# First products of a weight folding on both row halves of the matrix array, with one group of output weights moved ahead of the second products

## The reference

```python
q_hk = (hidden_q @ Wq.T).reshape(b, s, H, K)              # H = 16, K = 128
q_big = jnp.einsum('bshk,hkq->bshq', q_hk, w_kc_q)        # q = 192
q_r = jnp.einsum('bshq,hqr->bhsr', q_big, W_qr)           # r = 64
k_r = jnp.einsum('bld,hdr->bhlr', kv_rope, W_kr)          # d = 64
scores = jnp.einsum('bhsr,bhlr->bhsl', q_r, k_r)
attn = jax.nn.softmax(scores, axis=-1)
ctx_c = jnp.einsum('bhsl,bld->bhsd', attn, kv_rope)
ctx_lat = jnp.einsum('bhsd,hkd->bshk', ctx_c, w_kc_kv)
out = ctx_lat.reshape(b, s, H * K) @ Wo.T
```

## Time and profile before

| what | us |
|---|---|
| median of 3 runs | 1159.86 |
| lowest and highest of them | 1150.75, 1166.39 |
| the profiled execution, by the device time | 1156.2 |
| the profiled span | 1154.3 |
| of it, the folding phase | about 21 |

### The profile page before, as it was taken

The page is one execution under the profiler, slowest core; times in us unless marked ns, Lnnn a source line. Parts: engine busy times, 40 slices in busy tenths (PEclk is TensorE's granted clock), DMA queues, the critical chain, the costliest instruction groups (busy, mean ns, idle before and its releaser), DMA issues. The chain is left out here.

```text
span 1154.3 us, 32206 instructions
## 1 busy us (share of the span) xinstructions
PE 1093.3 (95%) x12466; PEld 835.1 (72%) x12467; DVE 707.1 (61%) x1804; ACT 452.4 (39%) x1329; POOL 300.6 (26%) x390
## 2 busy tenths in 40 slices
PE   7898999999999999999978999999998899899996
PEld 6776878878878668988756767767766688556664
DVE  6897755554646475545437888888885687422221
ACT  2453443443435222221135555555642566222221
POOL 1701532323132200000001212212213555334442
PEclk9899999999999999999999999999998999799999
DMA  8631211111111118000202332322324743312221
GB/s 257 185 86 39 74 45 44 54 28 55 27 55 30 35 43 245 1 0 0 50 7 67 78 81 74 87 77 65 92 79 155 210 112 85 102 29 34 37 27 10
DMA packets 72494, 82.55 MB, mean 72 GB/s; under 512 B 28910, under 2 KB 57231, under 8 KB 71916
## 3 DMA queue, kind: packets, MB, share of 16 engines
q1 hardware_dynamic: 64124, 62.33, 20.5%
q0 software_dynamic: 8304, 19.32, 6.4%
HBM read 64.91 MB, written 18.53 MB: 72 GB/s over the span
## 5 line engine op out<-in xcount | busy, mean ns | idle before, releaser
L1775 ACT ACTIVATE xattn_exps<-xattn_ps_s,xattn_top 128x256 f32<-128x256 f32 x256 | 117.8, 475 | 84.9 <-DVE xattn_top L1839 84.9
L776 PEld LDWEIGHTS attn_ps_q<-attn_xnT,w_b_q 128*128 128x128 f32 x1024 | 120.2, 195 | 12.6 <-issue 12.6
L776 PE MATMUL attn_ps_q<-attn_xnT,w_b_q 128*128 128x128 f32 x1024 | 124.8, 278 | 0.0
L830 PE MATMUL attn_ps_out<-w_b_o,attn_oT 128*128 128x256 f32 x480 | 106.6, 380 | 2.6 <-DVE all_x L1011 1.5
L830 PEld LDWEIGHTS attn_ps_out<-w_b_o,attn_oT 128*128 128x128 f32 x480 | 90.0, 190 | 16.1 <-DVE all_x L1011 2.4
L884 ACT COPY attn_qT<-attn_ps_q 128x512 f32<-128x512 f32 x64 | 38.1, 595 | 148.8 <-PE attn_ps_q L776 148.8
L1846 DVE STREAM_TRANSPOSE xattn_expsT<-xattn_exps 128x1024 f32<-128x1024 f32 x64 | 79.5, 1242 | 25.9 <-ACT xattn_exps L1775 25.8
L1836 DVE TENSOR_REDUCE xattn_raw_top<-xattn_ps_s 128x4 f32<-128x1024 f32 x64 | 77.3, 1207 | 15.9 <-PE xattn_ps_s L1666 15.8
L1643 PEld LDWEIGHTS xattn_ps_o<-xattn_xnT,all_d_a 128*128 128x128 f32 x512 | 62.1, 198 | 17.8 <-ACT xattn_exps L1775 7.2
L1608 POOL TENSOR_TENSOR xattn_ctxT<-xattn_weighed_sum,xattn_inverse 128x256 f32<-128x256 f32 x60 | 41.9, 729 | 126.6 <-DMA xattn_inverse<-xattn_inverse_rows 126.6
L1666 PE MATMUL xattn_ps_s<-all_c,xattn_qT 64*32 64x256 f32 x2048 | 69.8, 382 | 2.8 <-ACT xattn_exps L1775 2.8
(11 more groups left out here) (360 smaller groups left out, 2256.3 us busy)
## 6 DMA issues: line engine op xcount, KB each, us to landing
all_c<-roped_kT SPq DMA_DIRECT2D x32, 256.0 KB, 3.8
xattn_inverse<-xattn_inverse_rows SPq DMA_DIRECT2D x30, 256.0 KB, 4.0
attn_k_raw<-in_ctx SPq DMA_DIRECT2D x64, 64.0 KB, 2.0
roped_kv<-attn_k_kv SPq DMA_DIRECT2D x16, 256.0 KB, 2.1
roped_kT<-attn_k_turned SPq DMA_DIRECT2D x64, 64.0 KB, 1.7
all_c<-roped_kv SPq DMA_DIRECT2D x16, 256.0 KB, 2.9
moe_gate<-in_f_gate SPq DMA_DIRECT2D x8, 512.0 KB, 8.5
moe_up<-in_f_up POOLq DMA_DIRECT2D x8, 512.0 KB, 4.9
```

The costliest lines, as they stand in the source:

```text
L776: last = nc.tensor.matmul(ps_q[g % 2][:, h * P:(h + 1) * P], wq[:, c, head * DH:(head + 1) * DH], xnT[u][:, c, :], start=(c == 0), stop=(c ...
L830: last = nc.tensor.matmul(bank[:, 0:DIM], of_heads[:, h, :, :].rearrange("p b q -> p (b q)"), wo[:, h, :], start=(h == 0), stop=(h == HEAD ...
L1775: nc.scalar.activation(exps[g % 2][:, nkeys * k:nkeys * (k + 1)], ps_s[g % 2][:, nkeys * k:nkeys * (k + 1)], ACT.Exp, bias=top[u][:, n:n + ...
```

## The change

The products of group 0 stay on partitions 0 to 63, those of group 1 are laid on partitions 64 to 127, and one function issues both groups in turns. `raw_qr` and `raw_kr` become 128 partitions high and half as long, each loaded in two transfers, so nine transfers count for `got_d` instead of seven. `r1_made` is raised once, behind all 32 matmuls. PE's order loses the second `first_products`, and `out_weights(2)` moves from behind `turn_second(0)` to ahead of `second_products(0)`; ACT's order follows.

```diff
-            def first_products(g):
+            def first_products():
                 for n in range(half):
-                    h = g * half + n
                     for j in range(2):
-                        last = mm(ps_r1[g][j][0:QC, n * DC:(n + 1) * DC], raw["qr"][:, h, j * QC:(j + 1) * QC], raw["kr"][:, h, :],
-                                  start=True, stop=True)
+                        for g in range(2):
+                            last = mm(ps_r1[g][j][0:QC, n * DC:(n + 1) * DC], raw["qr"][side(g), n, j * QC:(j + 1) * QC],
+                                      raw["kr"][side(g), n, :], start=True, stop=True)
                 last.then_inc(s["r1_made"], 1)
...
             out_weights(0)
-            first_products(0)
+            first_products()
             out_weights(1)
-            first_products(1)
+            out_weights(2)
             second_products(0)
             second_products(1)
             turn_second(0)
-            out_weights(2)
             out_weights(3)
             turn_second(1)
...
             for g in range(2):
-                dve.wait_ge(s["r1_made"], g + 1)
+                dve.wait_ge(s["r1_made"], 1)
...
             out_weights(0)
             out_weights(1)
+            out_weights(2)
             act.wait_ge(s["r2T_made"], 2)
             nc.scalar.copy(r2T[1][:, :, :].rearrange("p m n -> p (m n)"), ps_r2T[1][:, :]).then_inc(s["r2T_by_act"], 1)
-            out_weights(2)
             out_weights(3)
...
-            "qr": sb2("qr", [DR, HEADS, DCQ]),
-            "kr": sb2("kr", [DR, HEADS, DC]),
+            "qr": sb2("qr", [2 * DR, HEADS // 2, DCQ]),
+            "kr": sb2("kr", [2 * DR, HEADS // 2, DC]),
...
-            sp.dma_start(raw["qr"][:, :, :], d["d_wqr"]).then_inc(got_d, 16)
-            sp.dma_start(raw["kr"][:, :, :], d["d_wkr"]).then_inc(got_d, 16)
+            for g in range(2):
+                rows, heads = slice(g * DR, (g + 1) * DR), slice(g * HEADS // 2, (g + 1) * HEADS // 2)
+                sp.dma_start(raw["qr"][rows, :, :], d["d_wqr"][:, heads, :]).then_inc(got_d, 16)
+                sp.dma_start(raw["kr"][rows, :, :], d["d_wkr"][:, heads, :]).then_inc(got_d, 16)
...
-            fold_weights(nc, "fold", lambda n: scope(n, phase), moments, consts, ident, [(got_d, 7 * 16)], raw,
+            fold_weights(nc, "fold", lambda n: scope(n, phase), moments, consts, ident, [(got_d, 9 * 16)], raw,
```

## The result

| what | before | after |
|---|---|---|
| median of 20 runs each | 1160.51 us | 1154.49 us |
| lowest and highest | 1150.75, 1168.79 | 1148.10, 1161.41 |
| ratio, 95% interval | | 0.9949 [0.9932, 0.9966] |
| the profiled execution: device time, span | 1156.2, 1154.3 | 1152.66, 1150.9 |

The kernel is faster by 0.5%, 5.9 us with an interval of 3.9 to 7.9. The forecast was 2.9 us, half the measured gain; the measured time lies within the range of 1149 to 1165 us.

What follows compares the result with a forecast made beforehand. The prediction took PE to bound the folding, the one phase changed; -2.86 us for first products plus 0 for output weights and 0 for transfers took the 1159.9 us median to 1157.0 us, range 1149 to 1165.

Steps and rivals of the forecast that it cites:

- What bounds the phase: Folding, 21.2 us: PE, busy 20.36 us, sets its end; a microsecond off PE's stream shortens the phase by one.
- First products: Folding's first products: both row halves run at once, one merged run replaces two of 2.93 us, -2.86 us.
- "no overlap": Upper time bound for the first products: weight loads share one path, spacing stays 87 ns, gain 0.
- Output weights and waits: Folding: moving output weights costs 0, within 0.21 us either way; they cover DVE's first copies with 0.4 us to spare.
- Transfers: Raw loads: same bytes, two more issues, 1.1 us of SP time over 100 us ahead of the folding; cost 0.
- The sum: Whole kernel: -2.86 + 0 + 0 = -2.9 us, from a median of 1159.9 to 1157.0 us.
- the first reading: Busy time of the folding, 569.4 to 590.6 us, read at a granted clock of 1.00, the 2.4 GHz level.
- the term of the removed work: Folding's first products: one of two runs on PE disappears, -2.86 us.
- The halves do overlap: Rival on the first products: halves don't overlap, spacing stays near 87 ns, 0 gained, 1159.9 us; chance 8%.
- all their switches: Rival on the merged run: each row-half switch empties the array at 0.21 us, slower, 1163.5 us; chance 3%.
- no copy came late: Rival in the folding: part of the gain, 63 ns spacing or a copy late by under 1 us, 1158.3 us; 17%.
- The rival of the clock: Behind the folding's barrier: half-clock stretch costing 1.1 us vanishes or doubles, 1155.9 or 1158.1 us; chance 20%, half each.

Runs made afterwards that it cites:

- the old place: The changed kernel with the third output weights back behind the first turn, on PE and ACT, halves still in turns; 1155.34 us, ratio 0.9953.
- the serial kernel: The changed kernel with all first products of group 0 issued before those of group 1, so no turns; 1159.68 us, ratio 0.9993.
- the pattern: Kernel before and changed kernel, each folding opening issued ten times more, each followed by 40 full-product records; before's repetitions took 16.57 to 21.42 us.
- the padded kernel: The changed kernel with seven unread 128x256 products ahead of the folding's first output weights; 1158.07 us, ratio 0.9990.

## Why the prediction was right, and where it fell short

**What bounds the phase: right.** In every profile PE's runs follow one another from the phase's start to its last turns, but for the 0.45 us of the old place. The stream became 3.0 us shorter, and so did the phase.

**First products: right.** Forecast was one run of 2.93 to 2.99 us for two of 2.93; it is 2.94 us. The ratio of two that I took from the 64-row products of cross attention 0 holds for 96 columns of weights as well. The bound of "no overlap" is the serial kernel, 5.59 us; the turns are what separates them.

**Output weights and waits: right.** The move costs nothing and saves 0.66 us against the old place, most of it the wait of 0.45 us, forecast as 574.40 to about 574.9. Counted from the phase's start, the second products start 0.09 us and the first turn 0.14 us earlier than I laid out, by two start-to-start times: 1.78 in place of 1.88 us and 3.60 in place of 3.65. The first of them says that a change of shape does not cost the 0.21 us everywhere: sixteen records 0.105 us apart need 1.68, which leaves 0.10 here.

**Transfers: right.** The four loads were issued within 2.5 us and PE did not wait for them; the serial kernel has them all and gains nothing.

**The sum: 2.9 us forecast, 3.0 measured in the phase at full clock.** As a forecast of the median it is too small. The step that failed is the first reading: "at a granted clock of 1.00". That was one execution. Another of the same kernel had 10 us at half clock in the same place and paid 4.8 us. So the term of the removed work, 2.86 us, is too small by the stretches that such work brings on in a part of the executions. With 4.8 us in one of three profiles, or 1.6 us a repetition in the pattern, the gain comes to 3.0 + 1.6 = 4.6 us, a ratio of 0.9960, which lies in the interval of either measurement. That the products on one row half run into the lower clock where those in turns do not is shown; that just this makes up the difference of the medians is an estimate from few executions, the padded kernel could not settle it, and the rest of the program moves by as much from one execution to the next.

**The rivals.** The halves do overlap, 64 records with all their switches take 2.94 us where 32 took 2.93, and no copy came late. The rival of the clock looked at the wrong place: I put it behind the barrier, where PE stands still, and gave it both signs. There the stretch neither vanished nor doubled: the 32 query products took 5.04, 6.47 and 6.54 us in the profiles of the kernel before, 5.34 and 6.35 in those of the changed one. A stretch can sit in the removed run too, where PE is never idle, and there it has only one sign. The Trainium skill (TensorE: Matmul & The Clock Gate, Part 1) tells of a gate on the clock that goes by how busy PE has been. The rows with PE busy for 33.40 of 33.40 us at 0.50 do not agree with that, if busy is meant as the profile counts it.

The range, 1149 to 1165 us, rested on the spread of three runs, and the 20 runs of before spread over 18 us.

## What to carry to other kernels

Products that use 64 of the 128 rows can be laid on both halves and issued in turns, each into its own bank: here the pair cost what one had cost. Turns are needed in the queue itself, and the copies behind the merged run need other work ahead of their reader. Before pricing a stage at full clock, look at more than one execution of it, above all where a long run of PE uses only part of the array.

## What the runs showed of the hardware

- 224 records of 64-row products on one half, without idle time, ran at the 1.2 GHz level from 1.4 us behind their start on; 448 records with halves in turns ran at 2.4 GHz throughout.
- Once down, the clock stayed down: for 54 us through the extra products and most of the folding, of which the same products run at 1.00 in the earlier trace rows. In the repeated pattern it came back after 3.6 us once and after a little over 10 us three times, with full products behind.
- At the lower level a run of 32 first products takes 5.38 us in place of 2.93.
